# Twelve stages on one core: tokens kept on chip from the spectra to softmax attention, an early convolution on the vector engine, semaphores cleared by five engines

## The reference

```
x = x + L0_conv(gn(x))       # graph attention over width, then a state-space model over time
x = x + L1_conv(gn(x))       # token attention and a mixer in Fourier space
t = tokens(x)
t = t + L2_attn(ln(t))       # linear attention, 8 heads
t = t + L2_ffn(ln(t))        # 64 experts with the 8 top tokens each
t = t + L3_attn(ln(t))       # attention with softmax of q and k, 4 heads
t = t + L3_ffn(ln(t))        # a sigmoid recurrence over the tokens
```

```
xc, z = split(xt @ in_proj)
xconv = conv_b + sum(conv_w[:, k] * shifted(xc, k) for k in range(4))
xc = silu(xconv)
dbc = xc @ x_proj;  dt = softplus(dbc[..., :R] @ dt_w + dt_b)
h = exp(dt * A) * h + (dt * xc) * B      # a scan over time
```

## Time and profile before

| what | us |
|---|---|
| median of 3 runs | 4353.73 (4347.12 to 4355.51) |
| the profiled execution | 4349.91 |
| its span, first to last instruction | 4348.2 |

### The profile page before, as it was taken

One profiled execution on the slowest core, in us unless ns is written; L12 is line 12 of the kernel. 1 busy time (PEld: TensorE's weight loads), 2 busy tenths in 40 slices (PEclk: granted clock), 3 DMA queues, 4 the chain that ended last, 5 costly groups with the idle time before them and its releaser, 6 DMA issues. The chain is left out here.

```text
span 4348.2 us, 83291 instructions
## 1 busy us (share of the span) xinstructions
PE 3548.3 (82%) x29212; PEld 2313.0 (53%) x29212; DVE 3195.8 (73%) x6216; ACT 2647.0 (61%) x5167; POOL 2512.2 (58%) x2922
## 2 busy tenths in 40 slices
PE   7997489999999999999999878668874965558666
PEld 4775155555555555555555547436653633346545
DVE  3998088888888888888888844638985855069854
ACT  5886278777777777777877521016765626148552
POOL 3998577788778887878778310016765412012750
PEclk7999599999999999999999955777767967789688
DMA  3001100000000000000000041252212233750233
GB/s 83 26 26 31 26 6 11 21 21 16 16 21 21 18 14 21 21 21 11 21 21 16 16 129 40 83 194 66 77 43 65 66 100 83 249 160 1 71 86 112
DMA packets 388771, 231.31 MB, mean 53 GB/s; under 512 B 44720, under 2 KB 367736, under 8 KB 386296
## 3 DMA queue, kind: packets, MB, share of 16 engines
q1 hardware_dynamic: 388360, 225.98, 18.2%
HBM read 150.15 MB, written 75.76 MB: 52 GB/s over the span
## 5 line engine op out<-in xcount | busy, mean ns | idle before, releaser
L1137 DVE TENSOR_TENSOR_SCAN mam_hs<-mam_dA,mam_ps_b 128x1024 f32<-128x1024 f32 x512 | 1156.3, 2275 | 2.3 <-PE mam_ps_b L942 2.1
L956 PEld LDWEIGHTS mam_ps_h<-mam_ident,mam_hs 128*128 128x128 f32 x4096 | 461.0, 146 | 421.6 <-issue 417.8
L942 PE MATMUL mam_ps_b<-mam_DB,mam_dtxt 32*128 32x512 f32 x2048 | 583.4, 645 | 85.2 <-DVE mam_hs L1137 82.4
L1075 ACT ACTIVATE mam_dA<-mam_dt,mam_A 128x496 f32<-128x496 f32 x1024 | 649.5, 704 | 0.7
L1083 ACT COPY mam_hTb<-mam_ps_h 128x512 f32<-128x512 f32 x768 | 424.8, 583 | 317.6 <-PE mam_ps_h L956 313.6
L956 PE MATMUL mam_ps_h<-mam_ident,mam_hs 128*128 128x128 f32 x4096 | 585.8, 288 | 27.8 <-ACT mam_hTb L1083 26.6
L740 POOL TENSOR_SCALAR mam_tap<-mam_xcp,mam_cw 128x512 f32<-128x512 f32 x192 | 301.2, 1569 | 18.7
L1147 DVE COPY mam_hTb<-mam_ps_h 128x512 f32<-128x512 f32 x256 | 175.8, 687 | 172.9 <-PE mam_ps_h L956 172.9
L968 PE MATMUL mam_ps_y<-mam_hTb,mam_WC 128*32 128x128 f32 x8192 | 280.3, 278 | 0.4 <-issue 0.4
L968 PEld LDWEIGHTS mam_ps_y<-mam_hTb,mam_WC 128*32 128x32 f32 x8192 | 211.6, 110 | 123.5 <-issue 94.1
L942 PEld LDWEIGHTS mam_ps_b<-mam_DB,mam_dtxt 32*128 32x128 f32 x2048 | 156.7, 184 | 220.9 <-issue 217.9
(11 more groups left out here) (713 smaller groups left out, 8634.2 us busy)
## 6 DMA issues: line engine op xcount, KB each, us to landing
moe_wg<-in_L_ffn_weight SPq DMA_DIRECT2D x32, 1024.0 KB, 8.1
rnn_xr<-x SPq DMA_DIRECT2D x23, 512.0 KB, 6.0
l1y_wh<-mode_weights SPq DMA_DIRECT2D x16, 544.0 KB, 3.8
gat_hg<-in_x SPq DMA_DIRECT2D x16, 512.0 KB, 7.1
h<-gat_out SPq DMA_DIRECT2D x32, 256.0 KB, 2.3
mam_ht<-h SPq DMA_DIRECT2D x128, 64.0 KB, 2.1
mam_hr<-h SPq DMA_DIRECT2D x128, 64.0 KB, 2.0
mam_xt<-in_x SPq DMA_DIRECT2D x128, 64.0 KB, 2.1
```

The source lines that it names most:

```text
L942: last = pe.matmul(ps_b[w % 2][:, n, :], steps[r, g * P:(g + 1) * P], DB[r, g, :, :].rearrange("p s t -> p (s t)"), start=True, stop=True, ...
L956: last = pe.transpose(ps_h[n][:, q * P:(q + 1) * P], hs[:, w % 3, c:c + P], ident[:, :])
L1075: act.activation(dA[:, h, :, n, 1:], dt[:, i % 2, h, :].rearrange("p (q t) -> p q t", q=Q)[:, :, 1:], ACT.Exp, scale=A[:, h, n:n + 1]).the ...
L1137: dve.tensor_tensor_scan(hs[:, w % 3, :], dA[:, h, first:first + 2, :, :].rearrange("p q s t -> p (q s t)"), ps_b[w % 2][:, :, :].rearrang ...
```

## The change

1. `Scope.clear` deals the semaphores out to five engines, every fifth one to each.
2. In `mamba` SyncE issues the loads in another order: the tokens of turn 0, `xp`, `dtw`, `w_in`, `cw`, `A`, `ow` (these six are now `loaded`), six column loads (a semaphore of their own, `cols_in`), then the tokens of turn 1. The vector engine convolves turns 0 and 1, GpSimd the later ones.
3. The tokens stay in one SBUF tensor `xf` from `token_spectra` to `softmax_attention`: first with rows of 128 elements (`x1`), from `token_mixer`'s last step on with rows of 129 (`x2`, then `x`). `x2`, `x3` and `x4` in HBM are gone, with their loads, stores and the waits for them. `token_mixer` writes unit k of `x2` over memory that holds the first image of unit k + 1 of `x1`, so `finish` waits for the residual of unit k + 1 too. `linear_attention` and `routed_experts` add in place.
4. Work that needs the weights comes later in three stages: in `linear_attention` vector engine and ScalarE start at `made` 1 and wait for 2 where they use `bk_b` and `bqc`; in `routed_experts` the gate's weights are turned after the first unit's rows; in `softmax_attention` the weights are turned after the second tile's rows, and ScalarE copies them after the third `normalise`.
5. `normalised_tokens`, which nothing calls, is removed.

```diff
     def clear(self):
...
-                    for q in self.sems:
+                    for q in self.sems[0::5]:
                         sp.sem_clear(q)
+                @block.scalar
+                def _(act):
+                    for q in self.sems[1::5]:
+                        act.sem_clear(q)
+                @block.vector
+                def _(dve):
+                    for q in self.sems[2::5]:
+                        dve.sem_clear(q)
+                @block.gpsimd
+                def _(pool):
+                    for q in self.sems[3::5]:
+                        pool.sem_clear(q)
+                @block.tensor
+                def _(pe):
+                    for q in self.sems[4::5]:
+                        pe.sem_clear(q)
...
-        LOADS = 12
+        LOADS = 6
+        EARLY = 2
...
-            for i in range(2):
-                tokens_for(i)
+            tokens_for(0)
+            sp.dma_start(xp[:, :, :], x_proj.rearrange("(h d) r -> d h r", h=HV)).then_inc(loaded, 16)
+            sp.dma_start(dtw[:, :], dt_w).then_inc(loaded, 16)
             sp.dma_start(w_in[:, :], in_proj).then_inc(loaded, 16)
             sp.dma_start(cw[:, :, :], conv_w.rearrange("(h d) k -> d h k", h=HV)).then_inc(loaded, 16)
-            sp.dma_start(xp[:, :, :], x_proj.rearrange("(h d) r -> d h r", h=HV)).then_inc(loaded, 16)
-            sp.dma_start(dtw[:, :], dt_w).then_inc(loaded, 16)
...
-                    sp.dma_start(dst[:, h:h + 1], src[h * P:(h + 1) * P].unsqueeze(1)).then_inc(loaded, 16)
+                    sp.dma_start(dst[:, h:h + 1], src[h * P:(h + 1) * P].unsqueeze(1)).then_inc(cols_in, 16)
+            tokens_for(1)
...
-                    if turn(k + 2):
+                    if turn(k + 2) and k + 2 >= EARLY:
                         convolve(k + 2, 0)
...
+            act.wait_ge(cols_in, 16 * 2 * 3)
...
+            dve.wait_ge(cols_in, 16 * 2 * 3)
             dve.wait_ge(prepared, 1)
+
+            def convolve(i, h):
+                dve.wait_ge(xc_ready, 2 * i + h + 1)
+                acc = xs[:, i % 3, h, :].rearrange("p (q t) -> p q t", q=Q)
+                step(TS(acc, xcp[:, h, :, 0:T], cw[:, h, 0:1], None, ALU.mult))
+                for k in range(1, K):
+                    step(STT(out=acc, in0=xcp[:, h, :, k:k + T], scalar=cw[:, h, k:k + 1], in1=acc, op0=ALU.mult,
+                             op1=ALU.add))
+                dve.sem_inc(conv_first, 1)
...
+                if u in (2, 4) and turn(k + 2) and k + 2 < EARLY:
+                    convolve(k + 2, u // 2 - 1)
...
-        hg = s.sb("hg", [P, BT, C])
+        hg = xf[:, 0:BT * C].rearrange("p (t c) -> p t c", c=C)
...
-        xx, a, mm = (s.sb(n, [P, 2, R, C]) for n in ("xx", "a", "mm"))
+        a, mm = (s.sb(n, [P, 2, R, C]) for n in ("a", "mm"))
+        x1 = xf[:, 0:BT * C].rearrange("p (t c) -> p t c", c=C)
+        x2 = xf[:, :].rearrange("p (t c) -> p t c", c=C + 1)
...
-                pool.wait_ge(res_ready, k + 1)
-                TT(f[:, k % 4, :, :], f[:, k % 4, :, :], res[:, k % 4, :, :], ALU.add).then_inc(out_ready, 1)
+                pool.wait_ge(res_ready, min(k + 2, UNITS))
+                TT(x2[:, k * R:(k + 1) * R, 0:C], f[:, k % 4, :, :], res[:, k % 4, :, :], ALU.add).then_inc(out_ready, 1)
...
-                               in1=xx[:, k % 2, r, :], op0=ALU.mult, op1=ALU.add)
+                               in1=x1[:, k * R + r, :], op0=ALU.mult, op1=ALU.add)
...
-            dve.wait_ge(made, 2)
+            dve.wait_ge(made, 1)
...
-                if m >= 4:
-                    dve.wait_ge(stored[m % 4], 16 * (m // 4))
-                TT(out[:, m % 4, :, :], ps_o[:, :].rearrange("p (r c) -> p r c", r=R), xb[:, m % XR, :, :], ALU.add
-                   ).then_inc(out_ready, 1)
+                TT(tokens(m), ps_o[:, :].rearrange("p (r c) -> p r c", r=R), tokens(m), ALU.add).then_inc(out_ready, 1)
...
-            for w in range(UNITS):
-                g, n = divmod(w, NU)
-                if w >= 8:
-                    sp.wait_ge(xin[w % 8], 32 * (w // 8))
-                for q in range(2):
-                    sp.dma_start(x[:, images(w, q), 0:C], xv[2 * g + q, n]).then_inc(xin[w % 8], 16)
...
             for w in range(UNITS + 1):
                 if w < UNITS:
                     turn_rows(w)
+                if w == 0:
+                    gate()
...
             for w in range(UNITS + 2):
                 if w < UNITS:
                     normalise(w)
+                if w == 0:
+                    gate()
...
-            for m in range(UNITS):
-                g, n = divmod(m, NU)
-                for q in range(2):
-                    sp.wait_ge(added, 2 * m + q + 1)
-                    sp.dma_start(ov[2 * g + q, n], x[:, images(m, q), 0:C]).then_inc(stored[(2 * m + q) % 4], 16)
...
                     if first:
-                        pe.wait_ge(w_ready, 1)
+                        turn_weights()
                         first = False
...
+                if n == 1:
+                    act.wait_ge(w_done, 1)
+                    act.copy(wT[:, :, :], ps_x[:, :].rearrange("p (j c) -> p j c", j=4)).then_inc(w_ready, 1)
...
-    x1, x2, x3, x4, x5 = (dram(f"x{n}", shape) for n in range(1, 6))
+    x1, x5 = (dram(n, shape) for n in ("x1", "x5"))
```

More of the change, by code:

```diff
@@ L815, in _ @@
                         spread_c(k, 3)
-                if u == 4 and turn(k + 2):
+                if u == 4 and turn(k + 2) and k + 2 >= EARLY:
                     convolve(k + 2, 1)
@@ L2290, in _ @@
                     load(k + 3)
-                k = due(w, 180)
-                if k is not None and k + 2 < UNITS:
-                    load_residual(k + 2)
-                k = due(w, 494)
-                if k is not None:
-                    sp.wait_ge(out_ready, k + 1)
-                    sp.dma_start(ov[k], f[:, k % 4, :, :]).then_inc(stored[k % 4], 16)
-            for j in range(4):
-                sp.wait_ge(stored[j], 16 * (UNITS // 4))
         @block.gpsimd
@@ L2799, in tiles, with tokens @@
             return 0 <= n < N
+        def tokens(n):
+            return x[:, n * R:(n + 1) * R, 0:C]
         @block.sync
         def _(sp):
-            for n in range(4):
-                sp.dma_start(xb[:, n % XR, :, :], xv[n]).then_inc(xin[n % 8], 16)
             for dst, src in ((wk, Wk), (wq, Wq), (wv, Wv), (wo, Wo)):
@@ L3288, in _, with gate @@
         def _(pe):
-            pe.wait_ge(loaded, 48)
             pe.wait_ge(made, 1)
-            pe.transpose(ps_p[:, 0:E], gw[:, :], ident[0:E, 0:E]).then_inc(g_done, 1)
-            pe.wait_ge(g_ready, 1)
+            def gate():
+                pe.wait_ge(loaded, 48)
+                pe.transpose(ps_p[:, 0:E], gw[:, :], ident[0:E, 0:E]).then_inc(g_done, 1)
+                pe.wait_ge(g_ready, 1)
             def rows_are_in(w, q):
@@ L3414, in _, with gate @@
         def _(act):
-            act.wait_ge(g_done, 1)
-            act.copy(gT[:, :], ps_p[:, 0:E]).then_inc(g_ready, 1)
-            act.wait_ge(loaded, 48)
+            def gate():
+                act.wait_ge(loaded, 48)
+                act.wait_ge(g_done, 1)
+                act.copy(gT[:, :], ps_p[:, 0:E]).then_inc(g_ready, 1)
             def normalise(w):
                 act.wait_ge(nb_ready, w + 1)
-                act.wait_ge(xin[w % 8], 32 * (w // 8 + 1))
                 if w >= 2:
@@ L3779, in _, with turn_weights @@
         def _(pe):
-            pe.wait_ge(loaded, 64)
             pe.wait_ge(made, 1)
-            for j in range(4):
-                last = pe.transpose(ps_x[:, j * C:(j + 1) * C], wl[:, j, :], ident[:, :])
-            last.then_inc(w_done, 1)
+            def turn_weights():
+                pe.wait_ge(loaded, 64)
+                for j in range(4):
+                    last = pe.transpose(ps_x[:, j * C:(j + 1) * C], wl[:, j, :], ident[:, :])
+                last.then_inc(w_done, 1)
+                pe.wait_ge(w_ready, 1)
             def turn_rows(n):
```

166 lines of the change are left out of this document (42 added, 124 removed).

## The result

The changed kernel takes 4277.15 us (median of 4 runs, 4275.22 to 4282.28) beside 4353.06 us for the kernel before on the same chip: ratio 0.9833, 95% interval 0.9818 to 0.9847. Two later comparisons gave 0.9831 (0.9818 to 0.9845) and 0.9822 (0.9800 to 0.9844). That is 72 to 76 us by the medians, where the forecast had some 80, and 4277 where it had 4272 (4256 to 4296). The profiled execution has a span of 4280.6 us.

The account below looks back on a forecast made before the run. No engine bounds the whole: twelve stages run one after another, with waits at their starts, ends and clears. Terms 20.8 + 30.7 + 17.5 + 10.4 = 79.4 us off 4349.9 give 4270.5, adjusted to 4272 us; range 4256 to 4296.

Parts of the forecast that it names:

- Clears: Twelve clearing blocks between stages: 29.7 us to fall to 8.9 on five engines, gain 20.8 us (14.5 to 24.3).
- Clears don't divide: Rival: a clear on the slowest engine costs 0.33 us, so the 20.8 us vanish: 4293 us; chance 0.10.
- Start of `mamba`: Stretch before `mamba`'s first scan: loads and the convolutions of turns 0 and 1 together gain 30.7 us.
- Loads and turn 0: `mamba`'s opening: reordered loads gain 4.2 us (3.2 to 5); vector engine convolving turn 0 gains 12.6 (12 to 12.7).
- Turn 1: `mamba`: vector engine convolves turn 1, its projection starts 13.9 us earlier (8 if `c_in` is late by its full price).
- the second rival: `mamba`'s first scan is held by something else, exponentials or the `c_in` wait; 13.9 us go: 4286 us; chance 0.10.
- Ends: Store waits gone behind `token_mixer` (3.2 us), `linear_attention` (2.3) and `routed_experts` (12.0): 17.5 us together.
- Starts: Earlier starts of `linear_attention` (4.9 us), `routed_experts` (2.9) and `softmax_attention` (2.6): 10.4 us together.
- Slower by code loading: Rival: instruction fetches at 12 clearing places eat the gain from 6.6 us each; at 8 us, 4368 us; chance 0.03.
- A stage's steady part gets longer by more than 2 us: Sign of being wrong: any stage's steady part, left as it is, gets longer or shorter by over 2 us.
- if the turns' period changes: Sign of being wrong, in `mamba`: turns were to keep the pace of before from the first scan on.
- the step halfway down from the median to the profiled execution: Whole kernel: profiled execution gives 4270.5 us, the runs' median is 3.8 higher; going halfway gives 4272.

Follow-up runs that it names:

- The repeats: Both kernels run again unchanged: the changed kernel's medians were 4278.5 and 4273.7 us; the one run of the kernel before had 4341.9 us.
- the first form of the last kernel: Changed kernel plus clears dealt by pitch, constants later in `linear_attention`, gate behind second unit's rows, `softmax_attention` weights turned first: 4269.7 us, ratio 0.9825.

## Why the prediction was right, and where its terms were off

*Clears.* Right in kind, 2.8 us too large: 18.0 instead of 20.8. The value taken for the slowest engine was 100 ns a clear; TensorE takes 117, enters its block 0.12 us after the first engine, and so needs 11.7 us for its share instead of 8.9. The bounds of 56 and 171 ns held. "Clears don't divide" falls by the runs with the clears alone and undone.

*Start of `mamba`.* 29.9 us against 30.7. Loads and turn 0 were right to 0.2 us. Turn 1 gave 12.8 instead of 13.9: the first group of `dtx` was counted at its old distance, but it now waits 1.6 us for `c_in`, behind the convolution. The prediction named this place and priced it only in its low bound. It took two of the six two-input ops for slow; three were (1.64, 1.64 and 1.42 us beside GpSimd, 0.75 the others), and the tensor-scalar op of the second half, which began beside a GpSimd op too, took 1.04 us instead of 0.49. So the convolution ended at 491.4, and `c_in`, whose input was there at 490.3, started only at 491.56. The Trainium skill, SBUF — State Buffer, on the shared port pair of the vector engine and GpSimd, says that the one blocks the other when a vector op has two inputs in SBUF and the GpSimd op reads SBUF. The three slow ops, each beside a GpSimd op with two inputs in SBUF, agree; the trace shows their length, not the blocking itself. That the projection's gain reaches the first scan in full was right; the second rival falls.

*Ends.* 17.6 against 17.5. They were read from SyncE's last waits, and the run with the stores put back gives the same 12.0. The other two, 3.25 and 2.33 us, are read from the profiles alone; no run put those stores back.

*Starts.* 4.5, 3.4 and 2.7 us against 4.9, 2.9 and 2.6. In each the walk through the queues found the instruction that holds the start: `bk_b + 1`, the gate's transpose, the copy of `wT`. No run undid the starts of `linear_attention` and `softmax_attention` by themselves; what supports them is that moving the same instructions further moved the starts further. `softmax_attention` as a whole lasted 291.5 to 293.8 us in the three profiles that have it as it was and 287.6 to 287.8 in the three of the changed kernel, so 1.2 us or more came from its later part, which wasn't traced. Rows of 129 elements cost nothing where they are new, as the prediction assumed: four statistics take 0.87 us, a `normalise` 1.65 and `token_mixer`'s last add 2.34, as before.

*Slower by code loading.* The mechanism may well be there, the price isn't: the longest distance between two clears of one engine was 0.36 us in the changed kernel, and the latest that an engine entered a block was 0.43 us, where 6.6 us a place were needed to eat the gain. Each of these is followed by a packet on the instructions' queue, so a fetch is the likely cause, though no run shows that it is. Most of the 0.6 us that the prediction found over 56 ns a clear in the first block is one such pause, of 458 ns instead of 58. The Trainium skill, Runtime: NRT & Kernel Launch, on instruction fetch, says that a taken branch to code that isn't loaded must wait for a fetch; no run here shows a stall of the size that the rival needed.

*What the sum left out.* "A stage's steady part gets longer by more than 2 us" was named as a sign of being wrong. It came: 5.9 us each in the scans and in `token_mixer`. The repeats show the same spread in the kernel of before, so nothing shows it to be a property of the change. The forecast's steps stand; what failed is the assumption under that sign, that a steady part repeats within 2 us. It repeats within 10, and the granted clock moves with it. The sign "if the turns' period changes" did not come: an undisturbed turn is 61.4 us in both kernels. The forecast lies 5.2 us below the measured median; its sum was 3.3 us too large, and 1.9 us are the step halfway down from the median to the profiled execution. The medians put the gain at 72 to 76 us and can't test terms of 3 us, so the fit of the total is in part luck; the terms rest on their stages. Some of the recorded arithmetic is off, without weight: by its own steps the range would be 4255 to 4295, its high end has 14.5 us for turn 1 that stand nowhere, and its chances give the range more than the 0.85 that it names.

## What to carry to other kernels

A stage's end and start are read from the last wait and from the instruction that heads each queue; walked with the durations of the old trace, they came out within 0.5 us outside `mamba`, and within 0.8 us for the start of `mamba` as a whole. When work is dealt to engines in equal parts, the slowest at that kind of instruction sets the time: deal by measured pitch. Work that is moved off a start because it "needs the weights" must be checked against when the weights land: here the gate was better left first.

## What the runs showed of the hardware

- A semaphore clear costs 58 ns on SyncE, 66 to 71 on ScalarE, 71 on GpSimd, 83 on the vector engine, 117 on TensorE, from start to start, with all five at it. With SyncE alone it was 58 as well: the other four don't slow it. The other engines weren't tried alone.
- Single pauses of 0.35 to 0.47 us stand between two clears in some blocks (six in 462 clears on SyncE), each followed 1.0 to 1.4 us after its start by an 8 KB packet on the instructions' queue.
- The same kernel's executions differ by up to 27 us of 4270 (4253.4 to 4280.0 in the first form of the last kernel, 4262.4 to 4282.3 in 14 executions of the changed one), and single stages by 10 of 430; TensorE's granted clock moves with them. A term under 5 us is to be read from the place in its stage where it arises, not from the kernel's time.
- 32 stores of 256 KB in a row kept the 16 DMA engines 98% busy at 285 GB/s, 0.9 us each; behind adds that came every 0.62 us, the wait for them ended 12 us later than without them.
- A half's convolution of 128x512 takes 2.85 us on the vector engine (0.49 and three times 0.75) where GpSimd took 10.7.
